# Three of sixteen maxima matmuls moved ahead of the values product, and the last key block moved behind the values' projections, in a fused attention and mixture-of-experts kernel

## The chip, the cores and the metric

The kernel runs on one core of one Trainium2 chip. The metric is the time of one execution on the device in microseconds (us), as the median of three runs.

## What is computed

The input x has 4 batches of 256 tokens of width 128. Each token attends to a context of 1601 rows of width 96 of its own batch, with 8 heads of 64, and the result is added to x. Then a feed-forward part with one shared expert and 8 routed experts (two chosen per token) is added too. Cut to what matters here:

```python
q = heads(layernorm(x) @ Wq); k = heads(ctx @ Wk); v = heads(ctx @ Wv)
attn = softmax(q @ k.T / 8)
x = x + (attn @ v) @ Wo + bo
# then x + shared_expert(layernorm(x)) + sum of the two best of 8 experts, weighted
```

## The kernel before, in words

The attention runs in 16 **pairs**, numbered n = 0 to 15: batch b = n // 4, and in it a pair p of two heads (n % 4). A pair's 1601 keys are cut into 13 chunks of at most 128, and these into 7 **units** (u = 0 to 6) of two chunks, the last of one chunk with 65 keys. For the projections and the maxima the keys are cut differently, into 4 **blocks** of 402.

Every engine walks through one list of steps that the function `plan` writes (lines 41 to 117), and each takes from it what it has to do, in that order. The steps of pair n that matter here are these.

* `("ring", ("max", ...))`: one **maximum**. TensorE multiplies 128 queries of one head (half h = 0 or 1 of the rows, 64 rows) with one block of 402 keys (line 1111), and VectorE reduces the 402 products to one maximum per query (line 914). A pair has 16: 4 blocks x 2 query tiles x 2 heads, in the order h = 0, 1, 0, 1, and so on. Below M0 to M15 are a pair's sixteen. They are made for pair n + 1 while pair n's scores are made.
* `shift`: the negated maxima go by small DMAs into a row that TensorE adds to the next pair's scores.
* `scores` of a unit, S0 to S6: two matmuls with that row (line 1161, half 1 then half 0), then for each chunk three matmuls of each half, again 1 then 0 (line 1170). ScalarE takes the exponential (line 797). The units use PSUM banks 0 to 3, two at a time, so unit n + 2 waits for the exponential of unit n.
* `sums` and `spread`: the sums of the pair before (lines 1049, 893, 753) and their inverses (lines 1057, 760, 858).
* `k` and `q`: the projections of the keys, blocks K0 to K3, and of the queries, for pair n + 2 (lines 1019 to 1021). ScalarE rounds them (line 745) and VectorE subtracts to get the low part (line 911).
* `v`: at n = 4, 8 and 12 the 13 projections of a new batch's values, which ScalarE copies out (line 773).
* `xn`, `y`, `xt`, `router`: at n = 1 the transposes of the other batches' normed x (two steps); at n = 5, 9, 13 the output projection y; at n = 6, 10 the transposes xt of the normed result; at n = 11 the router. VectorE takes each out of PSUM (lines 839 and 840 for xn and xt, 927 for y, 940 for the router).
* `add`: VectorE finishes the pair's sum of exponentials (lines 485, 486), after GpSimd's five additions (lines 481, 483).
* `values`: 52 matmuls with the exponentials (line 1186), 26 per head.

All steps called `ring`, apart from the keys of pairs from 2 on, take turns in the PSUM banks 4, 5 and 6. The bank is chosen at build time:

```python
            if w[0] == "k" and n > kinds.index("scores"):
                ...
                continue
            bank = min(range(lowest, O_BANK), key=lambda i: held.get(i, -1))
            ring_banks.append(bank)
            ring_last.append(held.get(bank))
            held[bank] = k
```

`lowest` is 4 here and `O_BANK` is 7. Before TensorE writes such a step's bank, it waits until the bank's last step was taken out (`ring_free`, line 1039: `pe.wait_ge(*taken(ring_list[ring_last[k]]))`). VectorE counts the steps it has taken in one semaphore, in the order of the list; ScalarE counts the values' projections in another.

In the kernel before, TensorE's order around pair n is: M0 to M2 of n + 1, S0, M3, M4, S1, M5, M6, ... S5, M13, M14, S6, M15, sums, K0, q, spread, K1, K2, K3, the steps y, xt, xn or router where there are any, and then the values product.

Of the kernel before, what the change touches and what calls it, by code (L numbers as in the profile page):

```python
# [34 lines left out]
def key_units(chunks):  # L35

    return [list(range(c, min(c + 2, chunks))) for c in range(0, chunks, 2)]
# [3 lines left out]
def plan(batches, pairs, chunks, heads_per_pair, tiles, blocks, halves, experts):  # L41

    n_units = len(key_units(chunks))
    order = [(b, p) for b in range(batches) for p in range(pairs)]
    n_order = len(order)
    maxima = [[("ring", ("max", b, p, i, t, k)) for k in range(blocks) for t in range(tiles)
               for i in range(heads_per_pair)] for b, p in order]
    couples = [maxima[0][i:i + heads_per_pair] for i in range(0, len(maxima[0]), heads_per_pair)]  # L50

    def keys(n):

        if n >= n_order:
            return []
        b, p = order[n]
        return [("ring", ("k", b, p, 0)), ("ring", ("q", b, p))] + [("ring", ("k", b, p, k)) for k in range(1, blocks)]

    first, second = keys(0), keys(1)
    v0 = [("v0", c) for c in range(chunks)]  # L60
    pieces = [sum(couples[i:i + 2], []) for i in range(0, len(couples), 2)]
    out = first[:2] + [("wv", 0)] + first[2:3] + [("ctx0", 3)] + pieces[0] + first[3:4] + v0[:2] + pieces[1]
    out += first[4:] + v0[2:4] + [("m", 0)] + pieces[2] + v0[4:6] + pieces[3]
    out += [("shift", order[0])] + [("stats", t) for t in range(1, batches)]
    rest = v0[6:]
    out += rest[:2]
    for i, x in enumerate(second):
        out += [x] + rest[2 + i:3 + i]
    out += rest[2 + len(second):]

    for n, (b, p) in enumerate(order):
        ahead = maxima[n + 1] if n + 1 < n_order else []
        out += ahead[:3]
        for u in range(n_units):
            out.append(("scores", (b, p, u)))
            out += ahead[2 * u + 3:2 * u + 5]
            if n == n_order - 1 and u in (0, 2):
                out.append((("sums", "spread")[u // 2], order[n - 1]))
            if u == 2 and p == 2 and b:
                out.append(("norm", b - 1))  # L80
        if ahead:
            out.append(("shift", order[n + 1]))

        vs = [("ring", ("v", b, c)) for c in range(chunks)] if p == 0 and b else []
        projections = keys(n + 2)
        if 0 < n < n_order - 1:
            out.append(("sums", order[n - 1]))
            projections = projections[:2] + [("spread", order[n - 1])] + projections[2:]
        if vs:
            for i, x in enumerate(projections or vs[:1]):  # L90
                out += ([x] if projections else []) + vs[2 * i:2 * i + 2]
            out += vs[2 * len(projections or vs[:1]):]
        else:
            out += projections
        if n == 0:
            out += [("normal", t) for t in range(1, batches)]
        if n == 1:
            out += [("ring", ("xn", 0)), ("ring", ("xn", 1))]
        if b and p == 1:
            out += [("ring", ("y", b - 1)), ("roots", b - 1)]  # L100
        if p == 1 and b + 1 < batches:
            out += [("ctx", (b + 1, k)) for k in range(blocks)]
        half, full = b * halves // batches - 1, b and b % (batches // halves) == 0
        if b:
            out += [("ring", ("xt", b - 1))] * (p == 2)
            if full and p == 3:
                out += [("ring", ("router", half)), ("exp", half)]
            if b - 1 and (b - 1) % (batches // halves) == 0:
                out += [("rank", half)] * (p == 0) + [("ring", ("wrow", half))] * (p == 2)
        if n == n_order - 2:  # L110
            out += [("w2", e) for e in range(experts)]
        out += [("w1", k) for k, at in enumerate((0, 2, 3)) if n == at]
        out.append(("add", (b, p)))
        out += [("values", (b, p, u, j)) for u, unit in enumerate(key_units(chunks)) for j in range(len(unit))]
        if n == n_order - 2:
            out += [("w2_low", e) for e in range(experts)]
    return out
# [51 lines left out]
def build(nc, x, ctxT, Wq, Wk, Wv, Wo, bo, router_w, router_b, sw1, sb1, sw2, sb2, rw1, rb1, rw2, rb2, out):  # L169
# [26 lines left out]
    assert D == P and 2 * DH == P and 0 < REST <= W4  # L196

    steps = plan(B, PAIRS, CH, 2, T, BLOCKS, NHALF, NE) + plan_experts(E, HK, NHALF, (B - 1, PAIRS - 1))
    ring_list = [w for kind, w in steps if kind == "ring"]
    ring_no = {w: k for k, w in enumerate(ring_list)}  # L200
# [1068 lines left out]
```

## Time and profile before

| | us |
|---|---|
| median of 3 runs | 413.12 (412.89 to 413.26) |
| the profiled execution, its own time | 414.8 |
| its span from first to last instruction | 412.9 |
| TensorE busy | 404.6 (98%) |
| TensorE weight loads busy | 334.7 (81%) |
| GpSimd busy | 270.3 (65%) |
| VectorE busy | 267.0 (65%) |
| ScalarE busy | 248.2 (60%) |

The mean granted clock of TensorE is 0.996 of full speed. Busy times of TensorE overlap: a matmul is listed from its start to a modelled end, so the distance from one start to the next tells more than a length. "PEld" is TensorE's weight load, "PE" its matmul, "DVE" VectorE, "ACT" ScalarE, "POOL" GpSimd.

### The profile page before, as it was taken

How to read it: one execution, taken by the hardware profiler on the slowest of the kernel's cores; microseconds unless marked ns; L12 is line 12 of the kernel's file. 1: busy time of each engine (PE TensorE's matmuls, PEld its weight loads, DVE VectorE, ACT ScalarE, POOL GpSimd, SP SyncE). 2: the span in 40 equal slices, each digit the busy share in tenths (PEclk: the TensorE clock that was granted, in tenths of full speed). 3: DMA queues.
4: the chain of work that ended last, by engine and by line, in shares of the span. 5: the costliest groups of instructions: out<-in, count | busy, mean ns of one | idle time of the engine just before them, and what ended most of it. 6: DMA issues, size and time to landing. Idle time of an engine off the chain costs nothing.

```text
span 412.9 us, 9465 instructions
## 1 busy us (share of the span) xinstructions
PE 404.6 (98%) x3590; PEld 334.7 (81%) x3590; DVE 267.0 (65%) x565; ACT 248.2 (60%) x399; POOL 270.3 (65%) x182
## 2 busy tenths in 40 slices
PE   7999999999999999999999999999999999999996
PEld 6787888797878887979779878888697777878886
DVE  5986878586626766857347667873585747557644
ACT  5677556382865554638737455467381736789883
POOL 6429788897913988567319793847075890498881
PEclk9999999999999999999999999999999999999999
DMA  6600002000000020000000120000000003202400
GB/s 209 175 1 2 2 2 62 2 2 2 0 2 2 3 61 1 2 2 2 1 2 3 59 61 2 2 2 0 2 3 2 0 3 103 102 2 71 148 14 27
DMA packets 17140, 11.75 MB, mean 28 GB/s; under 512 B 10188, under 2 KB 14136, under 8 KB 17096
## 3 DMA queue, kind: packets, MB, share of 16 engines
q1 hardware_dynamic: 17096, 11.15, 10.1%
q8 instruction: 30, 0.49, 0.5%
q14 instruction: 14, 0.11, 0.1%
HBM read 10.55 MB, written 0.56 MB: 27 GB/s over the span
## 4 chain that ended last, share of the span: by engine, by line
PE 94%; ACT 2%; DVE 1%; issue 1%; DMA 1%; POOL 0%; ACTq 0%; DVEq 0%
PE ps L1186 23%; PE ps L1170 16%; PE ps L1019 11%; PE ps L1020 10%; PE ps L1021 10%; PE ps L1111 8%; PE ps L1161 6%; PE ps L1049 4%; PE ps L1057 2%; PE ps L1118 2%; ACT probs L797 1%; ACT xn L720 1%; DMA x_sb<-in_x_dram 1%; DVE xn L877 0%; PE ps L1134 0%
## 5 line engine op out<-in xcount | busy, mean ns | idle before, releaser
L797 ACT ACTIVATE probs<-ps 128x1024 f32<-128x1024 f32 (+1 forms) x112 | 105.7, 963 | 114.4 <-PE ps L1170 111.3
L914 DVE TENSOR_REDUCE maxes<-ps 128x1 f32<-128x402 f32 x256 | 132.5, 570 | 44.8 <-PE ps L1111 40.1
L483 POOL TENSOR_TENSOR work<-work,probs 128x1024 f32<-128x1024 f32 x60 | 142.8, 2380 | 4.7
L1186 PE MATMUL ps<-probs,v_sb 128*64 128x256 f32 (+1 forms) x832 | 94.3, 384 | 0.0
L481 POOL TENSOR_TENSOR work<-probs 128x1024 f32<-128x1024 f32 x15 | 36.0, 2398 | 87.4 <-issue 75.4
L1186 PEld LDWEIGHTS ps<-probs,v_sb 128*64 128x64 f32 (+1 forms) x832 | 58.8, 138 | 31.8 <-issue 3.9
L1170 PE MATMUL ps<-kq_hi,kq_lo 64*128 64x256 f32 (+1 forms) x416 | 70.1, 280 | 0.0
L1170 PE MATMUL ps<-kq_lo,kq_hi 64*128 64x256 f32 (+1 forms) x416 | 70.0, 279 | 0.0
L1170 PE MATMUL ps<-kq_hi 64*128 64x256 f32 (+1 forms) x416 | 69.8, 278 | 0.0
L911 DVE TENSOR_TENSOR kq_lo<-ps,kq_hi 128x402 fp32r<-128x402 f32 (+2 forms) x80 | 41.7, 543 | 35.2 <-ACT kq_hi L745 33.8
L1111 PE MATMUL ps<-kq_hi 64*128 64x402 f32 x256 | 60.2, 365 | 0.1
L1161 PE MATMUL ps<-shift_rows,ones_r 64*128 64x512 f32 (+1 forms) x224 | 54.7, 407 | 1.1 <-ACT probs L797 0.9
L1170 PEld LDWEIGHTS ps<-kq_lo,kq_hi 64*128 64x128 f32 (+1 forms) x416 | 53.1, 181 | 2.3
L699 POOL TENSOR_TENSOR kq_lo<-probs,kq_hi 128x512 fp32r<-128x512 f32 x32 | 40.5, 1292 | 21.1 <-ACT kq_hi L812 19.7
L1170 PEld LDWEIGHTS ps<-kq_hi 64*128 64x128 f32 (+1 forms) x416 | 53.6, 182 | 0.1
L1170 PEld LDWEIGHTS ps<-kq_hi,kq_lo 64*128 64x128 f32 (+1 forms) x416 | 53.4, 182 | 0.0
L1111 PEld LDWEIGHTS ps<-kq_hi 64*128 64x128 f32 x256 | 33.2, 185 | 10.6 <-issue 5.8
L745 ACT CAST kq_hi<-ps 128x402 fp32r<-128x402 f32 (+2 forms) x80 | 36.4, 471 | 6.3 <-PE ps L1021 4.5
L1161 PEld LDWEIGHTS ps<-shift_rows,ones_r 64*128 64x128 f32 (+1 forms) x224 | 26.0, 177 | 5.2 <-ACT probs L797 1.9
L773 ACT COPY v_sb<-ps 128x512 f32<-128x512 f32 (+1 forms) x39 | 22.8, 586 | 6.2 <-PE ps L1021 3.9
L1019 PE MATMUL ps<-ctxT_hi,w_all 96*128 96x402 f32 x64 | 24.4, 381 | 0.7 <-DVE kq_lo L911 0.4
L822 ACT ACTIVATE ps<-ps,biasT 128x512 f32<-128x512 f32 x32 | 20.8, 661 | 4.8 <-PE ps L1021 4.4
(151 smaller groups left out, 655.3 us busy)
## 6 DMA issues: line engine op xcount, KB each, us to landing
v_sb<-weight_rows SPq DMA_DIRECT2D x12, 256.0 KB, 3.8
raw<-in_ctx_T_dram SPq DMA_DIRECT2D x3, 600.4 KB, 4.6
work<-in_L_ffn_rw_dram SPq DMA_DIRECT2D x1, 1024.0 KB, 6.9
shift_rows<-neg_row SPq DMA_DIRECT2D x64, 0.5 KB, 2.0
raw<-weight_rows SPq DMA_DIRECT2D x4, 256.0 KB, 3.5
raw<-in_ctx_T_dram SPq DMA_DIRECT2D x3, 150.8 KB, 2.9
x_sb<-in_x_dram SPq DMA_DIRECT2D x1, 384.0 KB, 6.6
wo_sb<-in_L_xattn_Wo_dram SPq DMA_DIRECT2D x1, 256.0 KB, 8.0
```

The lines of the kernel that those rows point to most:

```text
L483: ops.tensor_tensor(acc, acc, pr, ALU.add).then_inc(summed, 1)
L699: g.tensor_tensor(hid_lo[:, w % SPLITS, :], activations(w), hid_hi[:, w % SPLITS, :].bitcast(F32), ALU.subtract).then_inc(hid_lo_ready, 1)
L797: nc.scalar.activation(dst, src, ACT.Exp, scale=SCALE).then_inc(probs_ready, 1)
L911: v.tensor_tensor(lo, src, hi.bitcast(F32), ALU.subtract).then_inc(ring_taken, 1)
L914: v.tensor_reduce(maxes[:, p % 2, i * T + t, blk:blk + 1], src[:, 0:BW], AX.X, ALU.max).then_inc(ring_taken, 1)
L1019: mm(dst, a_hi, b_hi, start=start, stop=False)
L1020: mm(dst, a_hi, b_lo, start=False, stop=False)
L1021: return mm(dst, a_lo, b_hi, start=False, stop=stop)
L1111: ins = mm(dst[:, 0:BW], q_hi[rows, pair % 4, t * P:(t + 1) * P], k_hi[rows, pair % 2, k0:k0 + BW], start=True, stop=True)
L1161: mm(banks[0:rows, h, 0:n_c * S].rearrange("p (j s) -> p j s", j=n_c), ones_r[dims, 0:rows], shift_rows[dims, p % 2, :].unsqueeze(1).to_br ...
L1170: ins = mm(banks[0:rows, h, j * S:(j + 1) * S], keys[dims], queries[dims], start=False, stop=(i == len(factors) - 1 and j == n_c - 1))
L1186: ins = mm(o_bank[DH * i:DH * (i + 1), :], v_sb[0:rows, c, h * DH:(h + 1) * DH], probs[0:rows, n % SLOTS, i, j * S:(j + 1) * S], start=(c ...
```

## The change

For every pair but the first, the three maxima M0 to M2 of pair n + 1 are no longer at the head of pair n. They stand one pair earlier: behind the projections (and behind y, xt, xn and router) of pair n - 1, and in front of its `add` and its values product. The slots between the units are filled from M3 on, so that M3 to M5 stand at the head, two follow each of S0 to S4, and nothing follows S5 and S6. In the three pairs with values' projections, these go ahead of the keys' projections, and K3 comes last.

```diff
     for n, (b, p) in enumerate(order):
         ahead = maxima[n + 1] if n + 1 < n_order else []
+        sent = 0 if n == 0 else 3
+        ahead = ahead[sent:]
         out += ahead[:3]
         for u in range(n_units):
             out.append(("scores", (b, p, u)))
@@ -87,9 +89,9 @@
             out.append(("sums", order[n - 1]))
             projections = projections[:2] + [("spread", order[n - 1])] + projections[2:]
         if vs:
-            for i, x in enumerate(projections or vs[:1]):
-                out += ([x] if projections else []) + vs[2 * i:2 * i + 2]
-            out += vs[2 * len(projections or vs[:1]):]
+            for i, x in enumerate(projections):
+                out += vs[2 * i + 1:2 * i + 3] if i else vs[:3]
+                out.append(x)
         else:
             out += projections
         if n == 0:
@@ -110,6 +112,8 @@
         if n == n_order - 2:
             out += [("w2", e) for e in range(experts)]
         out += [("w1", k) for k, at in enumerate((0, 2, 3)) if n == at]
+        if n + 2 < n_order:
+            out += maxima[n + 2][:3]
         out.append(("add", (b, p)))
         out += [("values", (b, p, u, j)) for u, unit in enumerate(key_units(chunks)) for j in range(len(unit))]
```

## Rows read from the trace of the kernel before

**Rows 1.** The page, part 1: busy time and share of the span.

```profile
PE 404.6 (98%) x3590; PEld 334.7 (81%) x3590; DVE 267.0 (65%) x565; ACT 248.2 (60%) x399; POOL 270.3 (65%) x182
```

**Rows 2.** The chain that ended last, in order of time: start, length, what.

```profile
74.94 5.76 PE ps L1186 x52
...
93.24 5.76 PE ps L1186 x52
```

**Rows 3.** The waits: engine, line, whom it waited for: us, times, longest.

```profile
PEld ps L1111 <- DVE maxes L914: 4.1, 17, 0.4
```

**Rows 4.** Timeline at the head of pair 5: start, length, instructions, idle before.

```profile
126.29 0.63 PE L1111 MATMUL ps<-kq_hi 64*128 64x402 f32 x3
...
126.59 0.57 PE L1161 MATMUL ps<-shift_rows,ones_r 64*128 64x512 f32 x2
...
126.78 1.55 DVE L914 TENSOR_REDUCE maxes<-ps 128x1 f32<-128x402 f32 x3 [5.74 <-PE ps L1111]
...
127.54 0.35 PE L1111 MATMUL ps<-kq_hi 64*128 64x402 f32 x1
127.60 0.28 PE L1170 MATMUL ps<-kq_hi,kq_lo 64*128 64x256 f32 x1
127.89 0.18 PEld L1111 LDWEIGHTS ps<-kq_hi 64*128 64x128 f32 x1 [0.22 <-DVE maxes L914]
127.89 0.45 PE L1111 MATMUL ps<-kq_hi 64*128 64x402 f32 x1
```

**Rows 5.** Timeline at the end of pair 5's scores.

```profile
132.82 1.03 ACT L797 ACTIVATE probs<-ps 128x1024 f32<-128x1024 f32 x1
...
133.82 0.35 PE L1111 MATMUL ps<-kq_hi 64*128 64x402 f32 x2
...
134.00 0.28 PE L1161 MATMUL ps<-shift_rows,ones_r 64*65 64x256 f32 x2
...
134.48 0.34 PE L1111 MATMUL ps<-kq_hi 64*128 64x402 f32 x1
...
134.75 1.05 PE L1049 MATMUL ps<-ones,work 128*128 128x1 f32 x8
```

**Rows 6.** TensorE's timeline in pair 5, unit 4.

```profile
131.64 0.41 PE L1161 MATMUL ps<-shift_rows,ones_r 64*128 64x512 f32 x2
...
132.61 0.34 PE L1111 MATMUL ps<-kq_hi 64*128 64x402 f32 x2
```

**Rows 7.** Timeline around the start of pair 3's values product.

```profile
92.71 0.34 PE L1020 MATMUL ps<-ctxT_lo,w_all 96*128 96x402 f32 x1
...
92.89 0.35 PE L1021 MATMUL ps<-ctxT_hi,w_all 96*128 96x402 f32 x1
93.17 0.41 PEld L1186 LDWEIGHTS ps<-probs,v_sb 128*64 128x64 f32 x6 [0.27 <-issue]
```

**Rows 8.** VectorE's timeline at the head of pair 3.

```profile
81.12 4.77 DVE L914 TENSOR_REDUCE maxes<-ps 128x1 f32<-128x402 f32 x9 [0.92 <-PE ps L1111]
```

**Rows 9.** Timeline behind the xn transposes of pair 1.

```profile
56.58 3.24 PE L1186 MATMUL ps<-probs,v_sb 128*64 128x256 f32 x28
...
58.79 0.42 DVE L840 TENSOR_TENSOR xnT_lo<-ps,xnT_hi 128x256 fp32r<-128x256 f32 x1
```

**Rows 10.** Timeline behind the xt transposes of pair 6.

```profile
159.60 2.16 PE L1186 MATMUL ps<-probs,v_sb 128*64 128x256 f32 x18
...
161.01 0.42 DVE L840 TENSOR_TENSOR xnT_lo<-ps,xnT_hi 128x256 fp32r<-128x256 f32 x1
```

**Rows 11.** Timeline behind the y product of pair 5.

```profile
140.64 0.87 PE L1186 MATMUL ps<-probs,v_sb 128*64 128x256 f32 x6
140.75 0.42 DVE L927 TENSOR_TENSOR x_sb<-ps,x_sb 128x256 f32<-128x256 f32 x1 [0.63 <-PE ps L1118]
```

**Rows 12.** Timeline behind the router of pair 11.

```profile
263.98 0.65 PE L1186 MATMUL ps<-probs,v_sb 128*64 128x256 f32 x4
264.09 0.19 DVE L940 TENSOR_TENSOR logit<-ps,rb_sb 128x32 f32<-128x32 f32 x1
```

## The prediction, before the kernel was run

> **What bounds the kernel now.** The first view is the page's busy times [rows 1]. TensorE is busy for 98% of the span and every other engine for two thirds or less, so whatever TensorE does or waits for is the time. The second view is the chain that ended last: it runs through TensorE, and an ordinary pair, from one values product to the next, takes 93.24 - 74.94 = 18.30 us [rows 2]. The third view is the waits. Few are TensorE's, but one returns in nearly every pair: the weight load of a maximum waits for VectorE's reduction, 17 times, 4.1 us in all [rows 3]. The fourth view is the timeline, which shows where. At a pair's head three maxima go out at once, because three banks are free [rows 4]. M3 starts at 127.54, still behind S0's matmuls. M4 needs the bank of M1. VectorE's first reductions start at 126.78 and take 1.55 us for three, so the second ends at about 127.83, and M4 starts at 127.89. With nothing to wait for, it would have started 0.12 after 127.60, at 127.72. So TensorE loses some 0.17 us there.
>
> This shows also the rule on which the forecast rests: a step in banks 4 to 6 waits for the step three places before it in the list of bank users (keys' blocks don't count, they use the scores' banks).
>
> **What the change takes out of the scores.** It removes no work; three maxima per pair leave the end of the scores (slots behind S5 and S6) in the 14 pairs n = 1 to 14. The head stays as it was: three maxima (now M3 to M5), S0, then two, of which the second waits for the second reduction. So the 0.17 us stays. At the end, two maxima side by side cost 134.00 - 133.82 = 0.18 us; the single one costs 134.75 - 134.48 = 0.27 us, of which 0.10 is the change to another kind of matmul, which the last score would then pay (402 columns side by side with nothing take 0.17) [rows 5]. TensorE's own saving is thus 0.18 + 0.17 = 0.35 us. But S6 needs the banks of S4, whose exponential ends at 132.82 + 1.03 = 133.85, so S6 can't move from 134.00 to 133.82, only to 133.87. If ScalarE's chain doesn't move, the gain is 0.13 + 0.17 = 0.30 us; that is the low end. The chain may move too. Before, the odd count puts the halves half a step apart in S0 and S1 (127.60 - 127.54 = 0.06 from a matmul of one half to the next of the other), after it the halves are in step again behind M7, so S1's last score comes some 0.1 us earlier, and the alternation of S(n), its exponential and S(n + 2) carries that on. With no wait at all in the stretch I count 7.77 us for TensorE (three maxima 0.30 + 0.17, five pairs of maxima 0.90, six units of 132.61 - 131.64 = 0.97 [rows 6], S6 0.48 + 0.10) against the 134.75 - 126.29 = 8.46 now, a gain of 0.69; the upper end that I believe is 0.58, where ScalarE's chain starts 0.1 earlier and S5 and S6 follow each other as it allows. I take 0.42 us per pair, nearer to the low end, 14 times: -5.9 us.
>
> **What it puts in front of the values.** M0 and M1 side by side and M2 alone, in the 14 pairs n = 0 to 13. At a head, M0 to M2 start at 126.29 and the shift matmul that runs beside M2 at 126.59 [rows 4]; M2 starts by my count 0.28 after M0, which is 0.10 more than two maxima side by side. Then M2's own 402 columns 0.17. The change from the keys' projection to the values, 93.17 - 92.89 = 0.28 against 92.89 - 92.71 = 0.18, costs 0.10 now and would be paid behind M2 instead [rows 7]. That makes 0.45 us where the first pair pays its 0.10, and 0.35 where it doesn't; nothing in the trace has a maximum right behind a projection. I take 0.44 us, since the head is the nearest row: +6.2 us. The Trainium skill (TensorEngine Tiling (Array Packing), Key Properties) says that changing the tiling mode drains the engine; by it both new borders would cost, 0.45 us per pair. The rows show 0.10 us at such a border, but also between two kinds of matmul with the same tiling, so they don't tell the two apart.
>
> The two together are 14 x 0.02 = +0.3 us: as good as nothing. VectorE's three reductions (3 x 0.52) fall under the values product of 5.76 us, in front of `add`; pair 3's first reduction found VectorE idle for 0.92 us behind `add` [rows 8], and the new ones run while `add` waits for GpSimd anyway. The shift's DMAs go out 1 us earlier, with a whole values product of slack either way.
>
> **What the new place waits for.** This is the large term. M0 to M2 stand behind xn, xt, y and the router, and take the bank that these have just filled. By the rule of three, M2 waits for the bank of whatever stands directly between q and M0, if it is one step (q, X, M0, M1, M2: M2 is three behind X), and with two steps M1 waits for the first and M2 for the second. Before, the values product stood between and hid VectorE's taking out.
>
> * Pair 1, xn: M2 waits for the second xn. VectorE takes it out until 58.79 + 0.42 = 59.21 [rows 9]. M2 would start at 56.58 + 0.28 = 56.86. Stall 2.35 us.
> * Pairs 6 and 10, xt: taken at 161.01 + 0.42 = 161.43, M2 due at 159.60 + 0.28 = 159.88: 1.55 us each [rows 10] (pair 10 repeats it). VectorE is late since K3's low part stands ahead of xt. Together 3.1 us.
> * Pairs 5, 9, 13, y: taken at 140.75 + 0.42 = 141.17, M2 due at 140.64 + 0.28 = 140.92: 0.25 us each, 0.75 us [rows 11] (the other two repeat it).
> * Pair 11, router: taken at 264.09 + 0.19 = 264.28, M2 due at 263.98 + 0.28 = 264.26: 0.02 us [rows 12].
> * Pairs 4, 8, 12: M2 waits for the copy of the last v. With K3 (three matmuls of 0.18) moved between, the copy of some 0.6 us behind v's end is just done: 0 to 0.1 us each. With K3 ahead of the v it would be some 0.5. I find no other wait in those pairs that the move lifts or makes. The next pair's S0 wants K3's low part, a values product later.
>
> Sum: 2.35 + 3.1 + 0.75 + 0.2 = 6.4 us. Behind a stalled M2 stands the whole values product, and nothing can go ahead of M2, since TensorE works in order. The later stretch can't give it back, as it isn't bound by `add` or GpSimd.
>
> **Order of the halves.** Between units the new order is score h = 0, M6 (h = 0), M7 (h = 1), shift (h = 1): twice the same half follows itself, where before halves always alternated. When both halves are in step, that costs nothing if the weights are loaded under the running matmul. The nearest row is a projection, all rows of the array, whose loads follow each other on the same rows: 0.18 us for 402 columns [rows 7], as fast as the columns alone, so I take nothing. The Trainium skill (TensorE: Matmul & The Clock Gate, Part 3: Packing small matmuls) says that a weight load overlaps a running matmul only when the row group differs, which speaks against the change; its Part 2 adds the background weight buffer, and the projections agree with that. The sum by the first rule is a rival below.
>
> **Sum.** +0.3 + 6.4 = +6.7 us. The profiled execution took 414.8 us, with a span of 412.9; the median of the runs is 413.12, and the steps carry over: 413.1 + 6.7 = 419.8 us. The ends: per pair the net is 0.35 - 0.58 = -0.23 to 0.45 - 0.30 = +0.15, so -3.2 to +2.1 us, with 5.9 to 6.9 us of stalls: 415.8 to 422.1.
>
> **Rivals.**
> 1. *The bank waits don't show* (the rule of three read wrongly, or VectorE reaches xn and xt sooner). The rows of pair 5's head speak for the rule. The time is then 413.1 + 0.3 = 413.4, between 409.9 and 415.2. It is this that ends on the faster side, once the scores give more than 0.44 + 0.06 = 0.50 us per pair and no stall eats it. Chance 0.08.
> 2. *Same half after same half costs.* Two such places behind each of five units, 14 pairs: 140. If each shows about half of a 0.18 us weight load [rows 4], 0.09 us, that is up to 12.6 us, part of it hidden by the waits of S3 to S6 for ScalarE; half of it gives 419.8 + 6.3 = 426 us. Speaks against: the projections' rows. Chance 0.08.
> 3. *The scores give all their waits back*: 0.69 us per pair instead of 0.42, 3.8 us better, 416.0 us. Speaks against: the head's wait stays, and so does ScalarE's time of over 1.03 us per unit [rows 5]. It would be faster only with stalls under 14 x (0.69 - 0.44) = 3.5 us. Chance 0.06.
>
> **Numbers.** The forecast has 0.78. Its own range 415.8 to 422.1, widened to 414.9 and 423.0 towards the first rival and the second. A difference of 0.2% (0.8 us) is about what a measurement of this kernel can tell from none. Faster by more than that comes from rival 1's lower half and a sliver of rival 3, 0.06; the same 0.04; slower 0.90.
>
> **What would show it.** Right: in the profile after, weight loads of line 1111 waiting for lines 840 (about 2.3 and twice 1.5 us) and 927 (0.25 us); no maxima behind S5; the stretch from a pair's head to the sums 0.3 to 0.6 us shorter; K3 to the values 0.45 us longer; an ordinary pair (3 or 7) still 18.3 us long. Wrong: those loads start at once, or the distance between units in S0 to S4 grows by 0.1 us or more, or ordinary pairs are shorter by over 0.3 us.

## The result, and the profile after

The changed kernel takes 428.12 us (median of 4 runs, 426.28 to 438.32); the kernel before, on the same chip, 413.19. The ratio is 1.0349, 95% interval 1.0295 to 1.0403. Ratios, here and below, leave out executions in a slower state that any of these kernels shows at times (here 438.32, and 421.11 of the kernel before), while medians and ranges hold all. The direction was forecast, but the forecast was 419.8 us with 423.0 as its high end, so more than half of the 15 us was missed.

The page of the changed kernel, against [rows 1]:

```profile
span 436.4 us, 9465 instructions
...
PE 423.3 (97%) x3590; PEld 343.8 (79%) x3590; DVE 267.9 (61%) x565; ACT 248.4 (57%) x399; POOL 270.0 (62%) x182
...
PEclk9999999999999999899999998999999999999999
```

The instructions are the same in number, and TensorE is still the bound. The profiled execution began slowly: its first values product starts at 47.79 us, before at 37.45. At 12 us its keys' projections start 0.34 us apart instead of 0.18, as they would at half clock; the clock's own record begins only at 30.6 us in this profile. The second profile of the changed kernel, two edits of it and one of the kernel before show such a start with its record, half clock for 17.1 us from about 11 us on, ahead of every moved step. So I compare pair by pair, from the start of one values product to the start of the next. From the first values product to the last the change costs 321.1 - 307.9 = 13.2 us. The row of the granted clock has a dip in the 17th slice and one in the 25th, which the row before doesn't have. (The kernel before has one fall too, of 3.4 us at 328.3 us, spread over two slices; it comes up again below.)

The waits of the changed kernel, against [rows 3] (lines are 4 higher than before; 840 is now 844, 927 is 931, 1111 is 1115, 1186 is 1190):

```profile
PE ps L1115 <- DVE xnT_lo L844: 4.7, 4, 1.4
...
PEld ps L1115 <- DVE x_sb L931: 1.2, 3, 0.4
```

A maximum now waits for VectorE taking out xn and xt, four times, and the weight load of one waits for y, three times. Those are the waits that the prediction named, and the list before has no such rows. The timeline of TensorE in pair 1, against [rows 9], shows the first two of the four:

```profile
66.67 0.44 PE L1115 MATMUL ps<-kq_hi 64*128 64x402 f32 x1
68.50 0.44 PE L1115 MATMUL ps<-kq_hi 64*128 64x402 f32 x1 [1.38 <-DVE xnT_lo L844]
69.37 0.44 PE L1115 MATMUL ps<-kq_hi 64*128 64x402 f32 x1 [0.43 <-DVE xnT_lo L844]
69.74 5.83 PE L1190 MATMUL ps<-probs,v_sb 128*64 128x256 f32 x52
```

M1 waits for the first xn, M2 for the second, and the values product stands behind both. In pair 6 there is one step, xt, and M2 alone waits. TensorE's timeline there, against [rows 10]:

```profile
173.93 0.39 PE L1127 MATMUL ps<-ident,xn 128*128 128x128 f32 x2
174.24 0.45 PE L1115 MATMUL ps<-kq_hi 64*128 64x402 f32 x2
176.13 0.45 PE L1115 MATMUL ps<-kq_hi 64*128 64x402 f32 x1 [1.45 <-DVE xnT_lo L844]
176.52 7.52 PE L1190 MATMUL ps<-probs,v_sb 128*64 128x256 f32 x52
183.97 0.64 PE L1115 MATMUL ps<-kq_hi 64*128 64x402 f32 x3
```

VectorE's timeline in the same place shows what it did meanwhile:

```profile
173.62 1.67 DVE L915 TENSOR_TENSOR kq_lo<-ps,kq_hi 128x402 fp32r<-128x402 f32 x3
175.21 0.41 DVE L843 CAST xnT_hi<-ps 128x256 fp32r<-128x256 f32 x1
175.66 0.42 DVE L844 TENSOR_TENSOR xnT_lo<-ps,xnT_hi 128x256 fp32r<-128x256 f32 x1
```

The keys' low parts stand ahead of xt's high and low part; M2 starts 0.05 us after the latter ends (175.66 + 0.42 = 176.08).

The line of 176.52 says something that no step of the prediction has. The same 52 matmuls take 7.52 us here and 5.83 in pair 1. The windows of the changed kernel over this product (length; busy time of PE, PEld, DVE, ACT, POOL; granted clock; DMA):

```profile
174.00:176.50 2.50, 1.05 (x6) 0.44 (x4) 2.47 (x7) 0.56 (x2) 2.42 (x2) 1.00 0.00 0
176.50:178.00 1.50, 1.50 (x13) 1.00 (x14) 1.21 (x4) 0.00 (x0) 1.29 (x1) 0.80 0.00 0
178.00:180.00 2.00, 2.00 (x12) 1.07 (x10) 1.20 (x2) 0.00 (x0) 0.61 (x2) 0.50 0.02 4
180.00:182.00 2.00, 2.00 (x18) 1.27 (x16) 0.00 (x0) 0.00 (x0) 0.13 (x1) 0.79 0.00 0
182.00:184.00 2.00, 2.00 (x22) 1.11 (x18) 0.00 (x0) 0.00 (x0) 0.00 (x0) 1.00 0.00 0
```

TensorE was busy for 1.05 of 2.50 us around the wait, and just behind it the granted clock went from the level of 2.4 GHz to that of 1.2 GHz; two matmuls of the product start every 0.43 us there, at full clock every 0.21. The product lost 7.52 - 5.83 = 1.7 us. Pair 10 repeats it.

Pair by pair (us; "scores" is from 0.1 us behind the start of the last matmul of a values product to the first sums matmul, "projections" from there to the next values product):

| pair | scores, before to after | projections, before to after | values product slower by |
|---|---|---|---|
| 2, 3, 7 | 8.66 to 8.43 | 4.09 to 4.69 | 0 |
| 4, 8, 12 (v) | 8.65 to 8.42 | 13.15 to 13.71 | 0 |
| 1 (xn) | 8.66 to 8.41 | 4.92 to 7.98 | 0 |
| 6, 10 (xt) | 9.10 to 8.77 | 4.32 to 6.60 | 1.7 |
| 5, 9, 13 (y) | 8.66 to 8.43 | 5.88 to 6.85 | 0 |
| 11 (router) | 8.68 to 8.43 | 5.36 to 6.08 | 0 |
| 14 (nothing inserted) | 9.11 to 8.75 | 3.77 to 3.49 | -0.9 |

In pair 14 the fall of the clock lies in the kernel before.

An ordinary pair is 0.36 us longer (-0.24 + 0.60), 18.66 us, where the prediction expected it to stay at 18.3; pairs 6, 10 and 14 return somewhat more, 0.33 to 0.36 us. TensorE's timeline of pair 2 after shows both halves of this, against [rows 5] and [rows 7]; the first line is ScalarE's, from the same stretch:

```profile
82.03 1.03 ACT L801 ACTIVATE probs<-ps 128x1024 f32<-128x1024 f32 x1
```

```profile
83.11 0.34 PE L1165 MATMUL ps<-shift_rows,ones_r 64*65 64x256 f32 x2
...
83.73 1.05 PE L1053 MATMUL ps<-ones,work 128*128 128x1 f32 x8
...
87.57 0.35 PE L1025 MATMUL ps<-ctxT_hi,w_all 96*128 96x402 f32 x1
87.85 0.65 PE L1115 MATMUL ps<-kq_hi 64*128 64x402 f32 x3
88.43 5.83 PE L1190 MATMUL ps<-probs,v_sb 128*64 128x256 f32 x52
```

S6 starts 0.05 us behind the exponential that frees its banks (82.03 + 1.03 = 83.06), and takes 83.73 - 83.11 = 0.62 us to the sums instead of 0.75. From the keys' last projection to the values it is 88.43 - 87.57 = 0.86 us instead of 0.28.

### The profile page after: what moved, and what is told of

Same layout as the page of the kernel before. It is cut to its first block, busy times and chain, and to the rows that moved or that the text cites. A ratio compares the mean times of both kernels' runs of the same rounds, so it can differ in the third digit from the quotient of the medians.

```text
span 436.4 us, 9465 instructions
## 1 busy us (share of the span) xinstructions
PE 423.3 (97%) x3590; PEld 343.8 (79%) x3590; DVE 267.9 (61%) x565; ACT 248.4 (57%) x399; POOL 270.0 (62%) x182
## 4 chain that ended last, share of the span: by engine, by line
PE 93%; DVE 3%; ACT 2%; issue 1%; DMA 0%; POOL 0%; ACTq 0%; DVEq 0%
PE ps L1190 22%; PE ps L1174 15%; PE ps L1023 11%; PE ps L1024 10%; PE ps L1025 10%; PE ps L1115 9%; PE ps L1165 6%; PE ps L1053 4%; PE ps L1061 2%; PE ps L1122 2%; ACT probs L801 1%; DVE kq_lo L915 1%; ACT xn L724 1%; DMA x_sb<-in_x_dram 0%; DVE xnT_lo L844 0%
## 5 line engine op out<-in xcount | busy, mean ns | idle before, releaser
L918 DVE TENSOR_REDUCE maxes<-ps 128x1 f32<-128x402 f32 x256 | 132.4, 570 | 49.2 <-PE ps L1115 45.6
L1190 PE MATMUL ps<-probs,v_sb 128*64 128x256 f32 (+1 forms) x832 | 96.6, 390 | 0.4 <-DVE work L862 0.4
L1190 PEld LDWEIGHTS ps<-probs,v_sb 128*64 128x64 f32 (+1 forms) x832 | 60.5, 140 | 32.6 <-issue 6.6
L915 DVE TENSOR_TENSOR kq_lo<-ps,kq_hi 128x402 fp32r<-128x402 f32 (+2 forms) x80 | 42.0, 544 | 45.5 <-ACT kq_hi L749 37.5
L1115 PE MATMUL ps<-kq_hi 64*128 64x402 f32 x256 | 62.4, 392 | 5.3 <-DVE xnT_lo L844 4.7
L703 POOL TENSOR_TENSOR kq_lo<-probs,kq_hi 128x512 fp32r<-128x512 f32 x32 | 40.6, 1295 | 18.5 <-ACT kq_hi L816 17.1
L1023 PE MATMUL ps<-ctxT_hi,w_all 96*128 96x402 f32 x64 | 25.3, 396 | 0.6 <-ACT probs L801 0.3
```

Source lines behind the costliest of these rows:

```text
L703: g.tensor_tensor(hid_lo[:, w % SPLITS, :], activations(w), hid_hi[:, w % SPLITS, :].bitcast(F32), ALU.subtract).then_inc(hid_lo_ready, 1)
L915: v.tensor_tensor(lo, src, hi.bitcast(F32), ALU.subtract).then_inc(ring_taken, 1)
L918: v.tensor_reduce(maxes[:, p % 2, i * T + t, blk:blk + 1], src[:, 0:BW], AX.X, ALU.max).then_inc(ring_taken, 1)
L1023: mm(dst, a_hi, b_hi, start=start, stop=False)
L1115: ins = mm(dst[:, 0:BW], q_hi[rows, pair % 4, t * P:(t + 1) * P], k_hi[rows, pair % 2, k0:k0 + BW], start=True, stop=True)
L1190: ins = mm(o_bank[DH * i:DH * (i + 1), :], v_sb[0:rows, c, h * DH:(h + 1) * DH], probs[0:rows, n % SLOTS, i, j * S:(j + 1) * S], start=(c ...
```

## The experiments

The first result left three questions: whether the bank waits are the rule of three or something else; where the 5 us outside them come from; and whether the clock is a consequence of the waits. "Changed" and "before" name the two kernels. Times are medians, ratios are to the kernel before.

**The changed kernel again**, with no edit, for the spread and the second profile.

> The changed kernel once more, unchanged, for a profile without the late start of the first one (there the first values product began 10 us later than in the kernel before). Theory A (three causes): the bank waits at xn, xt and y, the clock at half speed for 3.4 us behind each of the two xt waits, and a net loss in every pair (0.60 us in front of the values, 0.24 back at the end of the scores). It expects 426 to 429 us, the first values product at 37.5 to 38.5 us, and every later pair's length as in the first profile to 0.1 us, apart from where the clock falls, which may move. Rival B (the loss spreads evenly over the pairs, 1 us in each, because the order of the halves or of VectorE's work costs everywhere) expects ordinary pairs near 19.3 us instead of 18.3.

431.5 us (426.7 to 442.09), ratio 1.0322 (1.0278 to 1.0367). Two of its four runs, 426.7 and 428.15, lie in the expected range; the first values product, expected at 37.5 to 38.5 us, started late again, at 45.6, with the clock at half from 10.9 to 28.0 us. The lengths of the pairs are those of the first profile to 0.1 us, but the clock fell behind pair 6's wait only; behind pair 10's, which is just as long, the values product took its usual 5.46 us from first to last start. So the waits are the kernel's, and whether the clock falls behind one differs from execution to execution.

**Early maxima only in the pairs without a bank wait**, and **only in the pairs with one**. The list of pairs is the only edit (n is the pair whose values product they precede):

```
-        sent = 0 if n == 0 else 3
+        sent = 3 if n - 1 in (0, 2, 3, 4, 7, 8, 12) else 0
-        if n + 2 < n_order:
+        if n in (0, 2, 3, 4, 7, 8, 12):
             out += maxima[n + 2][:3]
```

with the list (1, 5, 6, 9, 10, 11, 13) in the second.

> Three maxima early only in front of the seven values products with no xn, xt, y or router ahead of them (pairs 0, 2, 3, 4, 7, 8, 12). Theory A: 7 x (0.60 - 0.24) = +2.5 us, so 415.6 us, and no wait of a maximum for line 844 or 931. Rival B: half of the loss of 14 us, so 420 us.

> Three maxima early only in front of the seven values products that have xn, xt, y or the router ahead of them (pairs 1, 5, 6, 9, 10, 11, 13). Theory A: 7 x 0.36 = 2.5 us, 2.4 us at xn, 2 x 1.7 at xt, 3 x 0.4 at y, 0.1 at the router, and up to 2 x 1.7 for the clock: +9.6 us without the clock's part and +13.0 with it, so 423 to 426 us. Rival B: +7 us, 420 us.

Without waits 417.25 us (416.67 to 417.47), ratio 1.0075 (1.0049 to 1.0101): dearer by 1.6 us than expected, and with no wait for line 844 or 931 in its list and the clock full throughout. Moving three maxima costs even where nothing waits: 7 x 0.36 = 2.5 us are in the lengths above. The whole difference is 3.1 us (0.0075 x 413.2), and in the profiled execution the rest isn't the moved steps' doing: it is already 1.4 us late at its first score matmul (27.90 against 26.46 us), ahead of every moved step, with keys' projections 0.33 us apart instead of 0.18 in its first 10 us. With waits 424.72 us (422.85 to 426.3), ratio 1.0242 (1.0201 to 1.0284), as expected. Here the clock fell in pairs 1 and 10 (7.14 us from first to last start, instead of 5.46) and not in 6. The single runs line up with their granted clock: 422.85 at 1.0, 423.94 at 0.996, 425.49 and 426.3 at 0.992.

**Two early instead of three.** By the rule of three M0 and M1 alone reach the bank of a single step no more (M1 is two behind it); of the two xn, M1 still waits for the first.

```
+        sent = 0 if n == 0 else 2
...
+            out += maxima[n + 2][:2]
```

> Two maxima early instead of three, in the same 14 places. Then M1 is three places behind q where one step stands between, and not behind that step. Theory A: no wait at xt, y or the router and no fall of the clock there; at xn M1 still waits for the first xn, 1.5 us; two matmuls side by side in front of the values for 0.3 to 0.4 us per pair against some 0.24 back: +3 us, 416 us. Rival C (the wait at xt is VectorE's order of work, late K3 and xt, and would hit any maximum placed there): the waits stay, and it takes 422 us or more.

419.29 us (418.23 to 420.87), ratio 1.0129 (1.0095 to 1.0164). The waits of the kernel with two early:

```profile
PE ps L1115 <- DVE xnT_lo L844: 1.4, 1, 1.4
```

One wait is left of four, the one in pair 1 (projections 7.11 us, before 4.92); pair 6 takes 4.69. The rule of three is shown. The insertion costs 0.39 us instead of 0.60, but the scores give back only 0.18 instead of 0.24, and behind the one wait the clock fell again (and in pair 14, as in the kernel before). Hence 419 and not the expected 416.

**Kept busy through the waits.** TensorE multiplies ones into a bank that is free while M1 or M2 waits (nothing of the result changes, only work is added). If the clock falls because TensorE stands idle, it must not fall here.

```
+                    if w[0] == "max" and ring_last[k] is not None and ring_list[ring_last[k]][0] in ("xn", "xt"):
+                        pe.wait_ge(*sums_done(*divmod(w[1] * PAIRS + w[2] - 3, PAIRS)))
+                        for _ in range(4 if ring_list[ring_last[k]] == ("xn", 1) else 14):
+                            mm(ps[0:DH, O_BANK, 0:DH], ones[:], ones[:], start=True, stop=True)
```

> The changed kernel, with TensorE kept busy while it would wait for the bank of xn or xt: 14 small matmuls of ones in front of the second maximum of pair 1's early three and in front of the third in pairs 6 and 10, 4 in front of the third in pair 1, all into bank 7, which is free then. They add work and no result. Theory A (the clock falls to half for 3.4 us behind these waits, at a price of 1.7 us each time): no such fall behind pairs 1, 6 and 10, the waits' own time stays (2.4 and 2 x 1.7 us), and the kernel takes 1.7 to 5.1 us less than the changed one, 423 to 426 us, with less spread between its runs. Rival D (the values product behind the wait is slow for another reason, such as VectorE's and GpSimd's work beside it): the values product of pair 6 still takes 1.7 us longer than the others, and the time stays at 427 to 428 us or grows.

426.38 us (426.07 to 434.24), ratio 1.0292 (1.0245 to 1.0339). The values products of pairs 1, 6 and 10 all take 5.46 us, and three runs, all at a clock of 1.0, lie within 0.6 us of each other (426.07, 426.07, 426.68). The filling is a bit longer than the waits: pair 1 grows by 0.42 us, 6 and 10 by 0.25, 0.9 in all. Taken off, the changed kernel without a fall is at 426.07 - 0.9 = 425.2 us. Its own runs are at 426.28, 427.23 and 429.0, so the falls cost it 1 to 4 us. The three runs lie just above the expected 423 to 426 us, and a gain of one or two us on such a spread would be weak by itself; the clock is the better witness. In the profiles of the versions without filling (the changed kernel twice, the one with early maxima only in the pairs that wait, two early, and two that follow) 9 of 14 waits of about 1.4 us had a fall behind them; with the filling none of three, and the mean clock of 1.0 in its other three runs leaves no room for one.

**xt ahead of the last key block.** The moved K3 no longer stands ahead of xt, if VectorE's queue is the cause of the long wait.

```
+            if b and p == 2 and n + 2 < n_order:
+                projections = projections[:-1] + [("ring", ("xt", b - 1))] + projections[-1:]
```

> The changed kernel with xt in front of K3 instead of behind it (pairs 6 and 10). VectorE then takes xt out before K3's low part, and K3's 0.55 us stand between xt and M0. Theory A (M2 waits for xt's bank, and VectorE is late at it since K3's low part comes first): the wait falls from 1.45 us to 0.1 to 0.5 us per pair, the clock doesn't fall there, and the sum is 2 x 1.1 + up to 2 x 1.7 us less than the changed kernel: 422 to 426 us, with pairs 6 and 10 at 19.4 to 19.8 us instead of 20.9. If the wait had nothing to do with xt's bank, it would stay at 1.45 us.

429.52 us (424.89 to 433.86), ratio 1.0285 (1.0223 to 1.0347): the time doesn't tell it from the changed kernel (the expected 422 to 426 us was reached by one run of four). Its timeline in pair 6 does:

```profile
171.09 0.38 PE L1129 MATMUL ps<-ident,xn 128*128 128x128 f32 x2
...
171.95 0.45 PE L1117 MATMUL ps<-kq_hi 64*128 64x402 f32 x2
173.31 0.45 PE L1117 MATMUL ps<-kq_hi 64*128 64x402 f32 x1 [0.91 <-DVE xnT_lo L846]
```

The wait is 0.91 instead of 1.45 us, the projections 0.54 us shorter. I expected 0.1 to 0.5: VectorE still has the low parts of the first key blocks ahead of xt (its xt cast starts at 172.38, where the transposes are issued at 171.09). Pairs 6 and 10 take 20.4 us, not the expected 19.4 to 19.8. No fall of the clock is behind any wait of this profile. One of VectorE's three low parts was thus a third of the wait; the rest is those that were there anyway.

**Two maxima at the head and two behind each score unit** (on the kernel before, nothing sent early), to ask what the odd count of maxima at the head costs.

```
-        out += ahead[:3]
+        out += ahead[:2]
...
-            out += ahead[2 * u + 3:2 * u + 5]
+            out += ahead[2 * u + 2:2 * u + 4]
```

> The kernel before, with two maxima at a pair's head and two behind each of the seven units, instead of three, two behind each of six and one behind the last. No maximum moves to another pair. By theory A a lone maximum costs as much as two side by side, and the second maximum behind S0 waits 0.17 us for its bank because three were sent at the head. Here none is alone, and the first behind S0 needs only the first reduction: 0.2 to 0.4 us less per pair in 15 pairs, 3 to 6 us less than the kernel before, 407 to 410 us, unless ScalarE's chain of exponentials sets the pace of the units anyway (rival E: then S3 to S6 end as before and at most 1 us is gained).

414.21 us (413.8 to 422.58), ratio 1.0011 (0.9989 to 1.0033): I expected 407 to 410, and nothing was won. The distances between units did shrink, from 1.31, 1.24, 1.27, 1.23, 1.14, 1.20 us to 1.13, 1.13, 1.21, 1.14, 1.21, 1.13, yet the scores stay at 8.66 us. VectorE's timeline in this kernel, pair 3, and TensorE's at the end of the same scores:

```profile
88.48 8.99 DVE L914 TENSOR_REDUCE maxes<-ps 128x1 f32<-128x402 f32 x16 [1.42 <-PE ps L1111]
```

```profile
95.36 0.28 PE L1170 MATMUL ps<-kq_hi 64*65 64x256 f32 x2
...
95.72 0.80 PE L1111 MATMUL ps<-kq_hi 64*128 64x402 f32 x2
96.45 1.05 PE L1049 MATMUL ps<-ones,work 128*128 128x1 f32 x8
```

The 16 reductions run back to back for 8.99 us, longer than the scores, and the last two maxima wait for banks (0.80 us for two that take 0.35 elsewhere). So two things share the scores' length: the head of three, and behind it VectorE.

**Halves not alternating** (on the kernel before): all scores of one row half, then those of the other.

```
-                        for i, (keys, queries) in enumerate(factors):
-                            for h in (1, 0):
+                        for h in (1, 0):
+                            for i, (keys, queries) in enumerate(factors):
```

> The kernel before, with each chunk's six score matmuls ordered three of half 1 and then three of half 0, instead of alternating. If two matmuls of the same half can't overlap (second rival of the prediction, in its strongest form), a chunk takes about five instead of three and a half times 0.107 us, 0.17 us more, for 208 chunks: +35 us. If the order of the halves costs nothing, as the unchanged distances between units in the changed kernel suggest, it takes 413 us.

415.33 us (413.35 to 423.19), ratio 1.0019 (0.9985 to 1.0052), with the units 1.31, 1.24, 1.26, 1.23, 1.14, 1.22 us apart, as before. The expected 35 us didn't come. The trace says why this isn't quite the test that I had meant. TensorE's timeline in this kernel, pair 3:

```profile
103.43 0.30 PE L1170 MATMUL ps<-kq_hi 64*128 64x256 f32 x2
103.54 0.30 PE L1170 MATMUL ps<-kq_lo,kq_hi 64*128 64x256 f32 x2
103.67 0.30 PE L1170 MATMUL ps<-kq_hi,kq_lo 64*128 64x256 f32 x2
```

In the program the three matmuls of half 1 (high with high, high with low, low with high) stand ahead of the same three of half 0, yet two with the same operands start together, one of each half, every 0.12 us. That is the picture of the kernel before, whose timeline has the same three at 103.38, 103.49 and 103.61. The two halves run side by side in either order, and in either one a half's matmul follows another of its own half, as these lines of the kernel before show, where the load for the next matmul of a half starts with the running one:

```profile
103.38 0.28 PE L1170 MATMUL ps<-kq_hi 64*128 64x256 f32 x2
103.38 0.18 PEld L1170 LDWEIGHTS ps<-kq_lo,kq_hi 64*128 64x128 f32 x2
```

So the order of the halves in the program costs nothing here, in the one other order that was tried.

**The order of v and keys alone** (changed, nothing sent early: `sent = 0`, the inserted lines out).

> Only the second half of the change: the values' projections ahead of the keys' in pairs 4, 8 and 12, K3 last, no maximum early. Theory A: nothing waits there before or after, so 413 us, and those pairs at 27.3 to 27.4 us. If the new order had a price of its own, such as a wait for a bank between the values' projections, it would be at most 0.3 us in each of three pairs, 414 us.

413.83 us (412.81 to 424.86), ratio 0.9991 (0.9975 to 1.0007). Pairs 4, 8 and 12 take 27.35 to 27.40 us, before 27.34 to 27.38. The second half of the diff is free, as long as no maximum is sent early.

**Three early and two at the head** (changed).

```
-        out += ahead[:3]
+        head = 2 if sent else 3
+        out += ahead[:head]
...
+            out += ahead[2 * u + head:2 * u + head + 2]
```

> The changed kernel (three maxima early in all 14 places, with their waits at xn, xt and y), but with two maxima at the head of the scores instead of three; the 13 left stand as two at the head, two behind each of S0 to S4 and one behind S5. If the small return of the change (0.24 us per pair for three reductions of 0.56 us fewer) comes from the three at the head, whose banks make the second maximum behind S0 wait for VectorE, the stretch falls from 8.42 to 7.9 to 8.1 us and the kernel takes 4 to 7 us less than the changed one. If VectorE's reductions were all that counts, the stretch would not depend on how many stand at the head, and would stay at 8.4 us.

426.82 us (423.51 to 428.24), ratio 1.0312 (1.025 to 1.0374). The scores took 8.03 to 8.06 us, as expected 0.39 less than in the changed kernel (0.2 less in pairs 6, 10 and 14), 4.9 us in all. Little of it arrived at the end: the clock fell four times in the profile, in pairs 1, 6, 10 and 14. The best run is 423.51, at a granted clock of 0.991; the others lie between 426.69 and 428.24.

**Two early, two at the head, none in front of pair 1's values** puts the findings together: an even count everywhere, the third maximum not at the bank of xt, y or the router, and nothing behind the two xn.

```
+        sent = 2 if n not in (0, 2) else 0
+        head = 2 if sent else 3
+        out += ahead[:head]
...
+            out += ahead[2 * u + head:2 * u + head + 2]
...
+        if n + 2 < n_order and n != 1:
+            out += maxima[n + 2][:2]
```

> Two maxima early instead of three, but not at pair 1 (xn), and with two at the head and two behind each of S0 to S5, so that none is alone and VectorE has 14 reductions of 0.56 us in the stretch, 7.8 us, and not 16, 9.0 us, which filled the stretch in the version with two at the head. Theory F (VectorE's reductions set the length of the scores, and ScalarE's exponentials come close behind): the stretch from the end of a values product to the sums falls from 8.66 to 7.9 to 8.3 us; in front of the values it costs 0.4 us as with two early; net -0.35 to 0 us in 13 pairs, 409 to 413 us. If the stretch is held by ScalarE alone it stays above 8.4 us, as with three early, and the kernel takes 414 to 416 us.

411.9 us (410.24 to 420.42), ratio 0.9939 (0.9913 to 0.9964): 0.6% less than the kernel before, a small gain with an interval clear of 1, and in the expected range. Its TensorE timeline around pair 3's values product:

```profile
92.03 0.35 PE L1026 MATMUL ps<-ctxT_hi,w_all 96*128 96x402 f32 x1
92.31 0.45 PE L1116 MATMUL ps<-kq_hi 64*128 64x402 f32 x2
92.69 5.83 PE L1191 MATMUL ps<-probs,v_sb 128*64 128x256 f32 x52
98.45 0.45 PE L1116 MATMUL ps<-kq_hi 64*128 64x402 f32 x2
98.73 0.39 PE L1166 MATMUL ps<-shift_rows,ones_r 64*128 64x512 f32 x2
...
99.68 0.34 PE L1116 MATMUL ps<-kq_hi 64*128 64x402 f32 x2
99.86 0.39 PE L1166 MATMUL ps<-shift_rows,ones_r 64*128 64x512 f32 x2
```

Maxima come in twos, units follow after 99.86 - 98.73 = 1.13 us, the scores take 8.05 us instead of 8.66 (-0.61), the insertion costs 92.69 - 92.31 = 0.38 us. An ordinary pair takes 18.09 us instead of 18.30. Even in this profile the clock fell once (pair 14, where before it fell too).

Theory F had the length right and, by these numbers, the engine wrong: with 14 reductions in the stretch it is as long as with 13 in the version before (8.05 us both), so VectorE doesn't set it. ScalarE's timeline of the same scores, the seven exponentials:

```profile
99.89 2.16 ACT L802 ACTIVATE probs<-ps 128x1024 f32<-128x1024 f32 x2 [6.99 <-PE ps L1175]
102.23 2.16 ACT L802 ACTIVATE probs<-ps 128x1024 f32<-128x1024 f32 x2 [0.18 <-PE ps L1175]
104.58 2.64 ACT L802 ACTIVATE probs<-ps 128x1024 f32<-128x1024 f32 x3 [0.19 <-PE ps L1175]
```

From the first to the end of the last ScalarE is busy for 6.96 of 7.33 us. Before, the same chain had a gap of 0.40 us behind its first exponential, where the second maximum behind S0 waits. ScalarE's exponentials are thus the likely limit of the stretch with two at the head; no run took work from ScalarE to show it.

## Why the prediction was wrong in the time, point by point

**Right: the rule of three and its prices.** Each bank wait came where it was forecast. xn 2.46 us (forecast 2.35), xt 1.68 each (1.55), y 0.37 each (0.25), router 0.12 (0.02), v 0; each is the growth of the projections less the 0.60 of the insertion, 7.1 us in sum against 6.4. Each was forecast about 0.1 too low. Half of that is the time between VectorE's end and M2, 176.13 - 176.08 = 0.05, which the forecast left out; the rest I can't place. With two early the waits at the single steps go and the one at the two xn stays.

**Mis-sized: the insertion, 0.60 us and not 0.44.** The step is "That makes 0.45 us where the first pair pays its 0.10, and 0.35 where it doesn't". It counted 0.28 us from M0 to M2 and 0.17 for M2, and took the 0.10 between the last projection and the values as one that merely moves behind M2. The timeline after shows that 0.10 in both places: K3 to M0 takes 87.85 - 87.57 = 0.28 us, where projections follow each other after 0.18; from M0 over M2 to the values it is 88.43 - 87.85 = 0.58, half of it up to M2. So one 0.10 was left out, from K3 to M0; the remaining 0.05 I can't place. The Trainium skill (TensorEngine Tiling (Array Packing), Key Properties) says that changing the tiling mode drains the engine. The trace agrees so far as K3 and M0 differ in tiling and pay 0.10 us; whether the tiling is the reason, no run here tells.

**Mis-sized: the return, 0.24 us and not 0.42.** The step was "after it the halves are in step again behind M7, so S1's last score comes some 0.1 us earlier". It did not happen. The distances of S0 to S5 after are those of before to 0.02 us, and only S5 to S6 (1.20 to 1.10) and S6 to the sums (0.75 to 0.62) became shorter: the low end, 0.30, without ScalarE's chain moving, was the right account, less 0.06. What holds the chain back is the head of three: three early with two at the head took 8.05 us instead of 8.43. Whether its 0.39 us come from the second maximum behind S0, which waits for VectorE, or from the halves being half a step apart, no run separates. The 7.77 us that I counted from the first maximum at the head to the sums with no wait was nearly right, but for a head of two: measured like that, the runs with two at the head took 7.81 to 7.86 us in ordinary pairs.

**So "14 x 0.02 = +0.3 us: as good as nothing" was 14 x 0.60 - (11 x 0.24 + 2 x 0.33 + 0.36) = +4.7 us.** This is the step that failed most; the seven quiet pairs alone show it, and the bounds of the sum allowed only +2.1.

**Missing: the clock.** No step asked what TensorE's standing still would do to its speed. In the profile of before it was at full clock from the first values product up to pair 14, where it fell once. After, two waits of 1.4 us of idle cost 1.7 us each again behind them. That idleness is the cause, the run that was kept busy shows; why the same wait has it in one execution and not in the next stays open. Nor is 1.4 us the least that does it. In pair 14 of the kernel before TensorE stood idle for 0.72 us, and the clock fell 0.5 us later; its timeline and windows there:

```profile
327.83 0.78 PE L1057 MATMUL ps<-ident,repeated 128*128 128x128 f32 x4 [0.72 <-ACT repeated L753]
```

```profile
326.00:328.00 2.00, 1.28 (x10) 1.14 (x10) 1.31 (x5) 1.24 (x3) 1.92 (x2) 1.00 0.00 0
328.00:330.00 2.00, 2.00 (x12) 1.67 (x14) 0.91 (x3) 1.35 (x5) 1.92 (x2) 0.59 0.12 1
```

The version with the order alone has the same 0.72 us there and no fall. The Trainium skill (TensorE: Matmul & The Clock Gate, Part 1) tells of the clock's two levels, 1.2 and 2.4 GHz, and the granted clock of 0.50 in the windows of pair 6 agrees.

**The sum.** 4.7 + 7.1 = 11.8 us, on 413.1 is 424.9; the kept-busy kernel less its filling gives 425.2. One fall at 1.7 us on top makes 426.6, two make 428.3. The changed kernel's runs are 426.28 and 427.23 at a mean clock of 0.996, which is one fall of 3.4 us at half clock, and 429.0 at 0.992, which is two. Of what was missed above 419.8 us, 4.4 us are thus the two mis-sized steps, 0.7 the waits, and 1.7 to 3.4 the clock.

**The rivals.** The first (the waits don't show) is refuted by the waits' list. The second (same half after same half) is refuted by the distances S0 to S4, which would each have grown, and the halves taken apart add no cost either. The Trainium skill (TensorE: Matmul & The Clock Gate, Part 3: Packing small matmuls) lets a weight load overlap a running matmul only when the row group differs. The trace doesn't agree: the load of 103.38 above starts with a matmul of its own half, and the time with the halves apart, 1.0019 (0.9985 to 1.0052), shows no cost. The third (0.69 us back) was nearly to be had, 0.61 us, but only with two maxima at the head instead of three.

**Open.** Whether v's copy waits would have been 0.5 us with the old order, together with early maxima, wasn't tried. Whether the falls in before's pair 14 and in the changed kernel's 6 have one trigger, neither. No run of the changed kernel without any fall was measured, so its time at full clock is known only by the kept-busy kernel and by the sum.

## What to carry to other kernels

In a rotation of few banks, a moved instruction waits for whoever filled the bank so many places before it; list the neighbours at the new place before counting what the old place gives back, and see whether a long product stood between them as cover. Count every change of matmul kind at both ends of a moved group, and try how many of it should stand at the head of the next stretch: two instead of three were worth 0.39 us a pair here, where VectorE had room for it, and nothing where it hadn't. A wait of over a microsecond on the engine that is the bound costs twice where the clock falls behind it: price it with the next product at half speed, or give the engine something else to do there.

## What the runs showed of the hardware that I had not expected

- The granted clock fell from full to half behind 9 of 14 TensorE waits of about 1.4 us, in pairs 1, 6 or 10, and the 52 matmuls behind took 7.14 instead of 5.46 us from first to last start. With small matmuls in the wait it fell behind none of them. Behind an idle of 0.72 us it fell in one profile and not in another.
- Matmuls on the two row halves start together, every 0.12 us, whether the program alternates the halves or names three of one half before three of the other, at no cost (1.0019).
- Each border between matmuls of another kind costs 0.10 us (0.28 from start to start against 0.18), at projections to values before and at projections to maxima after; maxima to values take 0.28 too.
